# A running-maximum recurrence with the decay inside the scan, and three exponents from one difference

## The reference

```python
def step(carry, kv_t):
    p, q, o = carry
    kt, vt = kv_t
    no = jnp.maximum(o, u + kt)
    A = jnp.exp(o - no)
    E = jnp.exp(u + kt - no)
    y = (A * p + E * vt) / (A * q + E)
    no2 = jnp.maximum(w + o, kt)
    A2 = jnp.exp(w + o - no2)
    E2 = jnp.exp(kt - no2)
    return ((A2 * p + E2 * vt, A2 * q + E2, no2), y)
...
x = _layernorm(x + _L0_attn_ref(x, ...), axis=-1)
x = _layernorm(x + _L0_xattn_ref(16, 256, 512, w, u, x, ctx_2048), axis=-1)
x = _layernorm(x + _L0_ffn_ref(x, ...), axis=-1)
```

## Time and profile before

| | us |
|---|---|
| median of 3 runs | 1857.01 (1853.22 to 1861.23) |
| the profiled execution | 1865.38 |
| its span, first to last instruction | 1863.6 |
| PE busy | 1679.0 (90%) |
| DVE busy | 1612.3 (87%) |
| ACT busy | 1069.2 (57%) |
| POOL busy | 914.3 (49%) |

### The profile page before, as it was taken

One profiled execution on the slowest core, in us unless ns is written; L12 is line 12 of the kernel. 1 busy time (PEld: TensorE's weight loads), 2 busy tenths in 40 slices (PEclk: granted clock), 3 DMA queues, 4 the chain that ended last, 5 costly groups with the idle time before them and its releaser, 6 DMA issues. The chain is left out here.

```text
span 1863.6 us, 36120 instructions
## 1 busy us (share of the span) xinstructions
PE 1679.0 (90%) x11648; PEld 1528.0 (82%) x11648; DVE 1612.3 (87%) x3953; ACT 1069.2 (57%) x2994; POOL 914.3 (49%) x889
## 2 busy tenths in 40 slices
PE   5899989998989898989998989899999884789998
PEld 4788988897989897988898889898888873677786
DVE  4666799899999999898999998989999988799887
...
GB/s 239 191 211 173 112 96 169 87 66 103 168 94 65 94 171 103 64 82 168 117 52 84 176 120 52 74 173 132 54 73 152 143 57 74 57 46 68 80 69 46
DMA packets 108554, 202.95 MB, mean 109 GB/s; under 512 B 16848, under 2 KB 58320, under 8 KB 108368
## 3 DMA queue, kind: packets, MB, share of 16 engines
...
## 5 line engine op out<-in xcount | busy, mean ns | idle before, releaser
L759 POOL TENSOR_TENSOR RC<-QB,Cos 128x256 f32<-128x256 f32 x320 | 261.2, 816 | 577.5 <-DMA SW<-QB 476.1
L427 PE MATMUL bank<-Xh,W 128*128 128x256 f32 x1344 | 384.9, 286 | 38.1 <-DVE Xl L1035 26.4
L429 PE MATMUL bank<-Xh,W 128*128 128x256 f32 x1344 | 380.1, 283 | 0.0
L428 PE MATMUL bank<-Xl,W 128*128 128x256 f32 x1344 | 379.6, 282 | 0.0
L647 ACT ACTIVATE S<-S,NM 128x128 f32<-128x128 f32 (+1 forms) x512 | 229.0, 448 | 146.6 <-DVE NM L871 145.8
L427 PEld LDWEIGHTS bank<-Xh,W 128*128 128x128 f32 x1344 | 258.7, 192 | 41.7 <-DVE Xl L1035 30.3
L760 POOL TENSOR_TENSOR RSN<-SW,Sin 128x256 f32<-128x256 f32 x320 | 272.9, 853 | 0.0
L429 PEld LDWEIGHTS bank<-Xh,W 128*128 128x128 f32 x1344 | 259.4, 193 | 0.0
L428 PEld LDWEIGHTS bank<-Xl,W 128*128 128x128 f32 x1344 | 258.6, 192 | 0.0
L616 ACT ACTIVATE S<-S,RL 128x128 f32<-128x128 f32 (+1 forms) x512 | 203.6, 447 | 41.2 <-DVE RL L901 39.4
L427 PE MATMUL bank<-PTh,Vh 128*128 128x256 f32 (+1 forms) x512 | 138.1, 270 | 92.3 <-DVE OTl L866 91.9
...
## 6 DMA issues: line engine op xcount, KB each, us to landing
...
```

The costliest lines, as they stand in the source:

```text
L427: nc.tensor.matmul(dst, lhs[0], rhs[0], start=first, stop=False)
L428: nc.tensor.matmul(dst, lhs[0], rhs[1], start=False, stop=False)
L429: return nc.tensor.matmul(dst, lhs[1], rhs[0], start=False, stop=last)
L759: gp.tensor_tensor(RC[:, r % 2, :], QB[:, r % 2, :], Cos[:, :], ALU.mult)
```

## The change

The decay moves inside the scan: `MX[t+1] = max(k, MX[t]) + w`, so that `MX[t]` is already the decayed maximum. One difference, `D = k - MX[t]`, then gives three exponents: `E2 = exp(min(D, 0))`, `A2 = exp(-max(D, 0))`, and the weight of the present position relative to the state, `R = exp(min(D + u + w, LEAD))` with `LEAD` = 32. The result is `(PS + R * V) / (QS + R)`, without the pair of factors (A, E) that the reference has; a large R is bounded by `LEAD`, and the product of four denominators is scaled by `DOWN` = 2^-60 and scaled back. So the exponent of `AD`, `QS * AD` and `PS * AD` and their arguments aren't computed any more. The difference is taken on VectorE, not GpSimd. The tail is three slots shorter (`T_Y` 13, `T_END` 17), and the table of steps changes.

```diff
-T_Y = 16
-T_END = 20
+T_Y = 13
+T_END = 17
...
-STEPS_AT = {n: k for k, n in enumerate((264, 266, 268, 270, 275, 277, 279, 281, 283, 285, 289, 291))}
+STEPS_AT = {n: k for k, n in enumerate((262, 264, 266, 270, 271, 275, 277, 279, 281, 283, 286, 288))}
...
 # ScalarE
-                        above(act, d_done, tau)
-                        above(act, e2_arg, tau)
+                        above(act, y_done, tau)
...
-                    act.wait_ge(a2_arg, tau + 1)
-                    nc.scalar.activation(A2[:, :, :], A2[:, :, :], ACT.Exp).then_inc(a2_done, 1)
-                tau = at(7, 0)
-                if tau is not None:
                     act.wait_ge(e2_arg, tau + 1)
                     nc.scalar.activation(E2[:, :, :], E2[:, :, :], ACT.Exp).then_inc(e2_done, 1)
-                tau = at(8, 0)
...
-                    nc.scalar.activation(AD[:, :, :], AD[:, :, :], ACT.Exp).then_inc(ad_done, 1)
-                tau = at(9, 0)
...
+                tau = at(6, 1)
+                if tau is not None:
+                    act.wait_ge(a2_arg, tau + 1)
+                    nc.scalar.activation(A2[:, :, :], A2[:, :, :], ACT.Exp, scale=-1.0).then_inc(a2_done, 1)
+                tau = at(7, 0)
+                if tau is not None:
+                    act.wait_ge(r_arg, tau + 1)
+                    nc.scalar.activation(ED[:, :, :], ED[:, :, :], ACT.Exp).then_inc(r_done, 1)
...
 # GpSimd
-                    gp.tensor_tensor(E2[:, :, :], KT[:, :, :], MX[:, :, 1:T + 1], ALU.subtract).then_inc(e2_arg, 1)
...
-                    gp.tensor_tensor(QS[:, :, 0:T], QS[:, :, 0:T], AD[:, :, :], ALU.mult).then_inc(aq_done, 1)
...
-                    gp.tensor_tensor(AD[:, :, :], PS[:, :, 0:T], AD[:, :, :], ALU.mult).then_inc(ap_done, 1)
...
+                tau = tail_of(n, 8)
+                if tau is not None:
+                    pool.wait_ge(r_done, tau + 1)
+                    gp.tensor_tensor(KT[:, :, :], ED[:, :, :], VT[:, :, :], ALU.mult).then_inc(rv_done, 1)
                 tau = tail_of(n, 10)
                 if tau is not None:
...
+                    pool.wait_ge(ps_done, tau + 1)
+                    pool.wait_ge(rv_done, tau + 1)
+                    gp.tensor_tensor(EV[:, :, :], PS[:, :, 0:T], KT[:, :, :], ALU.add).then_inc(num_done, 1)
...
+            gp.tensor_tensor(UW[:, :], Ub[:, :], Wb[:, :], ALU.add)
...
 # VectorE
-                            last = v.tensor_tensor_scan(MX[:, c, 1:T + 1], Wb[:, c:c + 1].to_broadcast([P, T]), KT[:, c, :], NEG, ALU.add, ALU.max)
+                            last = v.tensor_tensor_scan(MX[:, c, 1:T + 1], KT[:, c, :], Wb[:, c:c + 1].to_broadcast([P, T]), NEG, ALU.max, ALU.add)
...
                 tau = at(5, 2)
                 if tau is not None:
                     dve.wait_ge(mx_done, tau + 1)
+                    v.tensor_tensor(KT[:, :, :], KT[:, :, :], MX[:, :, 0:T], ALU.subtract).then_inc(z_done, 1)
+                    above(dve, y_turned, TT * tau)
+                    dve.wait_ge(z_done, tau + 1)
+                    v.tensor_scalar(E2[:, :, :], KT[:, :, :], 0.0, None, ALU.min).then_inc(e2_arg, 1)
+                    v.tensor_scalar(A2[:, :, :], KT[:, :, :], 0.0, None, ALU.max).then_inc(a2_arg, 1)
+                tau = at(6, 1)
+                if tau is not None:
                     for c in range(KC):
-                        last = v.scalar_tensor_tensor(out=A2[:, c, :], in0=MX[:, c, 0:T], scalar=Wb[:, c:c + 1],
-                                                      in1=MX[:, c, 1:T + 1], op0=ALU.add, op1=ALU.subtract)
...
-                        last = v.scalar_tensor_tensor(out=AD[:, c, :], in0=KT[:, c, :], scalar=Ub[:, c:c + 1],
-                                                      in1=MX[:, c, 0:T], op0=ALU.add, op1=ALU.subtract)
...
-                    v.tensor_scalar(ED[:, :, :], AD[:, :, :], 0.0, None, ALU.min).then_inc(ed_arg, 1)
-                    v.tensor_scalar(AD[:, :, :], AD[:, :, :], 0.0, -1.0, ALU.max, ALU.mult).then_inc(ad_arg, 1)
...
+                        last = v.tensor_scalar(ED[:, c, :], KT[:, c, :], UW[:, c:c + 1], LEAD, ALU.add, ALU.min)
+                    last.then_inc(r_arg, 1)
...
-                    tau = at(10, 1 + half)
+                    tau = at(8 + half, 1)
...
-                    v.tensor_tensor(ED[:, 2, :], ED[:, 0, :], ED[:, 1, :], ALU.mult).then_inc(quad_done, 1)
+                    v.scalar_tensor_tensor(out=ED[:, 2, :], in0=ED[:, 0, :], scalar=DOWN, in1=ED[:, 1, :],
+                                           op0=ALU.mult, op1=ALU.mult).then_inc(quad_done, 1)
```

79 lines of the change are left out of this document (26 added, 53 removed).

## The result

| | before | after |
|---|---|---|
| median of 4 runs each, us | 1859.12 (1853.22 to 1866.18) | 1879.68 (1876.65 to 1881.5) |
| span of the profiled execution | 1863.6 | 1874.8 |
| PE busy | 1679.0 | 1680.9 |
| DVE busy | 1612.3 | 1522.7 |
| ACT busy | 1069.2 | 1046.1 |

The changed kernel takes 1.0107 of the time of the one before, with a 95% interval of 1.0068 to 1.0147: 1.1% slower, where the forecast said 2.3% faster. VectorE works 90 us less and GpSimd 124 us less, and none of it shows in the time. (The two profiled executions lie nearer to each other than the medians: before's is near the top of its runs and after's is the lowest of its own.)

What follows compares the result with a forecast made beforehand. The bound changes from slot to slot, each costing the larger of VectorE's time and its floor. Slots gave -2.3 us per period, -32 over 14 tails, plus -11 behind the heads: -43, so 1814 us, range 1766 to 1852.

Steps and rivals of the forecast that it cites:

- What bounds the kernel: In the head slots: neither engine is full; each slot costs the larger of VectorE's time and TensorE's floor.
- VectorE's total: Rival over the whole kernel: all VectorE savings come through, 5.7 us for each of 16 tails, 1766 us; chance 0.17.
- The floor of 4.46: TensorE's least time in a head slot with only the Q projection and nothing to wait for: 4.46 us.
- The floor of 5.85: TensorE's least time in slots 4 to 7 and 12 to 15, which add twelve matmuls: 5.85 us.
- slot 6: Head slot numbered 6 modulo 16: clamps leave, the whole QS scan enters; 6.6 us, a change of +0.9.
- The slower rival: Slots 6 and 8: GpSimd's multiplies by V delay OTl; +1.3 us per period, 1875 us; chance 0.09.
- The late rotations: Rotations queued behind each GpSimd multiply come late by about as much as its extra hold, 0.9 us each.
- Its two reasons against itself: At GpSimd's multiplies: GpSimd is idle for long parts of slots; VectorE issues the sum before the semaphore reaches GpSimd.
- The port: SBUF access: VectorE operations on two SBUF inputs and GpSimd ones reading SBUF exclude each other for a whole instruction.
- The 1.6 us per operation: Stretch that one full-tile GpSimd operation was taken to put on VectorE: 1.6 us.
- Slot 4: Difference and two clamps arrive on VectorE, with 0.1 for two waits on its own results: 6.05 us, +0.4.
- The end: Stretch behind the heads, with the last two tails: the full 5.7 us counts for each, -11 us.

Runs made afterwards that it cites:

- The place of one operation: Two kernels, PS halved and QS whole in slot 6, against the kernel before: GpSimd's multiply by V two slots after QS, 1804.3 us; in slot 6, 1843.8 us.

## Why the prediction was wrong

It forecast 1814 us in 1766 to 1852 and gave faster 0.79; the time is 1879.7. By its own steps, in us: the length of each group of slots as forecast and as measured (means of 14 periods), and the changes.

| slots | length forecast | length measured | change forecast | change measured |
|---|---|---|---|---|
| 0 to 3 | 19.1 | 19.6 | -0.6 | -0.6 |
| 4 | 6.05 | 7.12 | +0.4 | +1.6 |
| 5 | 5.85 | 5.37 | -1.45 | -1.7 |
| 6 | 6.6 | 9.46 | +0.9 | +3.8 |
| 7 | 7.9 | 8.13 | -0.7 | 0.0 |
| 8 | 6.85 | 5.05 | +1.25 | +0.4 |
| 9 | 4.8 | 5.39 | -2.7 | -2.4 |
| 10 and 11 | 10.7 | 9.87 | -0.6 | -1.0 |
| 12 to 15 | 25.2 | 25.3 | +1.2 | +1.2 |
| sum | 93.05 | 95.3 | -2.3 | +1.2 |

- **What bounds the kernel: right in the main.** The bound does change from slot to slot. VectorE's busy time per period was forecast at 81 and is 80.5. A sum over VectorE's total would have been worse still. The floor of 4.46 holds: no mean length of a slot with the Q projection alone is more than 0.25 under it in any kernel of the table. The floor of 5.85 is too high for single slots, since slot 5 takes 5.37 and slot 7 5.42 where nothing holds them.
- **The base.** The sum subtracts from the windows of one period, which add to 95.3 us; the mean of the 14 periods is 94.1. So 1.2 of the 3.5 us per period between forecast and measured change, 17 us in all, were lost before any mechanism came in; slot 7 had 8.6 in that period and 8.12 on the mean. There is a slip of addition too: the terms for slots 12 to 15 (twice 5.85 + 0.43, then 6.1 and 6.8) make 25.5 and not 25.2, which makes the sum -2.0 and the forecast some 4 us longer.
- **The prices of operations: right.** The clamp is 0.37 against 0.35 forecast, the difference 1.23 against 1.20, the scan with its operations exchanged takes what it did, and ScalarE's second exponent in slot 5 doesn't hold that slot (5.37).
- **The step that failed is slot 6**, +0.9 against +3.8. The sum took `QS` out of slot 7 and put its stretched partner, "the multiply by V on GpSimd now runs here, 1.6", into slot 7. It runs in slot 6, between `QS` and `OTl`; and the second multiply runs in slot 7, not in 8. Both were placed one slot late, though their lags, 7 and 8, say 6 and 7. Moving the 1.6 to slot 6 would not change the sum by itself. What it hid is the price at that place, which the pair of kernels under "The place of one operation" gives: `QS` alone takes slot 6 from 5.62 to 7.26, with TensorE and not VectorE full (+1.6, forecast +0.9), and the multiply takes it to 9.43 (+2.2, where the sum had nothing) and slot 7 from 5.42 to 7.01.
- **The slower rival.** The prediction had this mechanism there, with its place and a price of +1.3 per period (measured: +1.2) and 1875 us (measured: 1879.7), but gave it 0.09. The first multiply does what it says. That the number is so near is in part luck. The second multiply costs less than its full length, `Ql` at 1.83 instead of 0.42 in slot 7. The late rotations, half of the rival's price, are not seen in slots 6 to 8: the waits of VectorE for them lie in slots 1, 2, 12 and 13 and make some 0.8 per period. And its change is counted from the same long base. Its two reasons against itself failed for one cause. That VectorE issues the sum before the semaphore reaches GpSimd is true, by 0.16 us, and protects one sum; this slot has two, the second for K. That GpSimd is idle for long parts of a slot is why the multiply starts at once.
- **The port.** A sum of 0.419 us at the median takes up to 2.573 in this trace, and a multiply that has begun (814.99) is over (817.43) before the next sum runs. The page "SBUF — State Buffer" of the Trainium skill, section "Who interferes with whom", says that the order of issue decides who blocks, and that the other waits for the whole instruction. The trace agrees. The 1.6 us per operation that the sum used was a mean of four groups; this one, released by the end of `QS`, begins at the same point in each of the 14 periods, holds the second sum every time (2.57 instead of 0.42), and costs 2.15.
- **Slot 4**, +0.4 against +1.6: the new operations were priced right, but as if `Ql`, `RF` and the clamps stayed unstretched. The wait on the difference, counted at 0.1 for two, is right: 0.11 in the usual period.
- **Slots 7 and 8** follow from the same slip. Slot 7 was near its forecast in length (7.9 against 8.1) by luck, and for another reason: the stretch in it is the second multiply's, and it follows the stall of slot 6 with a granted clock of 0.78. Slot 8 got +0.4 instead of +1.25, as the second multiply isn't there.
- **The end**, -11 against -1.4. VectorE is busy 175.0 there against 187.3, as forecast, and the time isn't shorter. The same arithmetic in the old places has 7.5 less. The four kernels with the new table and `T_Y` end in 339.5 to 342.5, the eight with the new arithmetic and the old table in 331.3 to 338.6. So some 6 us of it went with the new places or the new table of steps; which of the two was not separated.
- **Where the gain went.** A gain of the size of the forecast's 43 us exists, 37 for the arithmetic with both scans in halves; that is a likeness of sizes and no proof of the sum, since the places differ. Between the changed kernel and one with `QS` in slot 6, `PS` in halves, the multiply later and the rest in the old places lie 75 us (1879.7 against 1804.3). The one order of operations in slot 6 is 39.5 of them where it was tried by itself; the other 36 came with the other new places and stay open one by one.
